# Row scatters from SBUF in place of lists in DRAM, and scores in three fp32r passes

## The reference, cut to what matters

```python
# attention, 16 heads of 16 features; kernel of 1 + s/4 + (s/4)^2/2, s = q.k
qf, kf = taylor_exp(q), taylor_exp(k)
A = jnp.tril(jnp.einsum('bhnd,bhmd->bhnm', qf, kf))
y = jnp.einsum('bhnm,bhme->bhne', A, v)
z = 1.0 / (jnp.einsum('bhld,bhld->bhl', qf, jnp.cumsum(kf, axis=2)) + EPS)
attn = (y * z[..., None]) @ Wo.T             # heads put side by side
# experts: 8, two for each token
top_w, top_i = jax.lax.top_k(xn @ Wg, 2)     # softmax over the two
y_e = (jax.nn.silu(xn @ W1[e]) * (xn @ W2[e])) @ W3[e]
moe = sum of the two chosen y_e, each times its weight
```

## Time and profile before

| | |
|---|---|
| median of 3 runs | 752.8 us (752.7 to 753.59) |
| profiled execution: time, span | 748.22 us, 746.5 us |
| PE busy, clock granted on average | 670.4 us (90%), 0.967 |
| DVE, ACT, POOL busy | 378.3, 318.9, 337.9 us |
| DMA moved | 46.77 MB, 63 GB/s |
| attention (to 389.8 us) and experts | 389.8 and 356.7 us |

### The profile page before, as it was taken

One profiled execution on the slowest core, in us unless ns is written; L12 is line 12 of the kernel. 1 busy time (PEld: TensorE's weight loads), 2 busy tenths in 40 slices (PEclk: granted clock), 3 DMA queues, 4 the chain that ended last, 5 costly groups with the idle time before them and its releaser, 6 DMA issues.

```text
span 746.5 us, 15613 instructions
## 1 busy us (share of the span) xinstructions
PE 670.4 (90%) x5315; PEld 502.1 (67%) x5315; DVE 378.3 (51%) x919; ACT 318.9 (43%) x468; POOL 337.9 (45%) x356
## 2 busy tenths in 40 slices
PE   3679999999998999887569999999999999999993
PEld 2435565656565655544258888888888888888882
DVE  4645656575756654354348744444444444444441
ACT  3355756566665656364237422333322333222330
POOL 1153544545352625243305655555545555545542
PEclk9899999999999999999679999999999999999997
DMA  6106053543516050003851233333333333333331
GB/s 211 37 1 86 17 32 97 40 104 38 107 31 84 16 43 16 15 2 42 252 225 29 52 59 58 58 59 58 58 54 55 51 59 59 58 54 55 58 52 21
DMA packets 37240, 46.77 MB, mean 63 GB/s; under 512 B 9520, under 2 KB 31424, under 8 KB 37168
## 3 DMA queue, kind: packets, MB, share of 16 engines
q1 hardware_dynamic: 21024, 25.71, 17.6%
q0 software_dynamic: 15712, 19.01, 15.8%
q10 hardware_dynamic: 432, 1.06, 0.4%
HBM read 27.50 MB, written 18.26 MB: 61 GB/s over the span
## 4 chain that ended last, share of the span: by engine, by line
PE 74%; DVE 12%; DMA 5%; issue 3%; another core or an unknown queue 2%; ACT 1%; POOL 1%; SPq 0%; DVEq 0%; POOLq 0%; ACTq 0%
PE banks L1007 26%; PE banks L1028 13%; PE banks L872 8%; PE banks L909 6%; PE banks L890 6%; PE banks L1016 4%; PE banks L953 3%; PE banks L918 3%; PE banks L938 2%; DMA lists_scr<-ids,slots 2%; DMA out<-yo,glist 2%; PE banks L996 2%; DVE yw L634 1%; DVE st L577 1%
## 5 line engine op out<-in xcount | busy, mean ns | idle before, releaser
L371 POOL TENSOR_SCALAR_AFFINE_SELECT T<-T 128x512 f32<-128x512 f32 x128 | 79.5, 637 | 173.3 <-ACT T L458 60.6
L411 POOL DMA_INDIRECT out<-yo,glist x71 | 114.1, 1607 | 81.0 <-DMA out<-yo,glist 39.0
L540 ACT ACTIVATE sTh<-banks 128x512 fp32r<-128x512 f32 x71 | 42.5, 598 | 193.6 <-PE banks L1016 193.6
L1007 PE MATMUL banks<-w12h,xgh 128*128 x284 | 118.7, 418 | 4.5 <-DVE xgl L821 4.5
L400 POOL DMA_INDIRECT xg<-xn_scr,glist x71 | 69.7, 981 | 106.7 <-DVE yo L833 94.8
L872 PE MATMUL banks<-Qs,Ks 32*128 32x512 f32 (+3 forms) x1024 | 100.5, 475 | 16.9 <-ACT T L463 8.3
L1007 PE MATMUL banks<-w12l,xgh 128*128 x284 | 112.4, 396 | 0.0
L1007 PE MATMUL banks<-w12h,xgl 128*128 x284 | 112.3, 396 | 0.0
L826 DVE TENSOR_TENSOR sTl<-banks,sTh 128x512 fp32r<-128x512 f32 x71 | 49.0, 691 | 116.7 <-ACT sTh L540 116.7
L450 ACT ACTIVATE T<-banks 128x1024 f32<-128x1024 f32 x64 | 62.0, 1021 | 53.1 <-PE banks L872 49.0
L872 PEld LDWEIGHTS banks<-Qs,Ks 32*128 32x128 f32 x1024 | 46.0, 187 | 51.6 <-issue 21.1
(11 more groups left out here) (157 smaller groups left out, 1133.4 us busy)
## 6 DMA issues: line engine op xcount, KB each, us to landing
w12r<-w SPq DMA_DIRECT2D x16, 512.0 KB, 8.2
xn_scr<-xb SPq DMA_DIRECT2D x8, 512.0 KB, 9.3
out<-xa SPq DMA_DIRECT2D x16, 256.0 KB
w3r<-w SPq DMA_DIRECT2D x8, 512.0 KB, 7.0
xa<-x SPq DMA_DIRECT2D x7, 512.0 KB, 4.4
xg<-xn_scr,glist POOLq DMA_INDIRECT x71, 2.8
out<-yo,glist POOLq DMA_INDIRECT x71, 3.8
lists_scr<-ids,slots POOLq DMA_INDIRECT x64
```

The source lines that it names most:

```text
L371: e.affine_select(out=v, in_=v, pattern=[[0, 4], [1, P]], compare_op=ALU.is_ge, fill=-1.0, base=0, channel_multiplier=-1).then_inc(s["g_mk ...
L411: e.indirect_dma_start(out, bass.IndirectOffsetOnAxis(glist[:, t:t + 1].bitcast(U32), 0), yo[:, t % 2, :], None, compute_op=ALU.add).then_ ...
L1007: i = e.matmul(banks[:, 2 * (t % 2) + m, :], a[:, k, :], w[:, bass.ds(expert[t] * 4 + (2 * k + m), 1), :], start=(k == 0 and n == 0), stop ...
```

## The change

**No lists in DRAM.** A row of xn, its eight gate weights and its token number now stand side by side in SBUF (`xb`, 272 words). POOL's `send` scatters each row to `xs_scr` by batch, expert and rank, twice, one indirect DMA for 128 rows, eight a batch; they stand singly between masks (`sends_after`). The stores of xn, the table, the wait on its entries and the read of the lists are gone. DVE works out which row of `xs_scr` each tile's row is (`tile_starts`, `tile_gaps`, `tile_rows`, `all_rows`, in the steps of batch 7). The scatter of results uses the row's own token number, copied with the weights (`xw`). Gates are worked out batch by batch.

**Scores.** q and k are kept as high and low parts, ACT making the high, DVE the low ones, and each group of columns takes three fp32r passes, in the same four row groups. Part 1 is 384 columns, part 2 twice 256 (where 128 would do for one).

**Beside it**: slots and DVE's work in them are arranged anew; buffers are laid out so that 8 weight units can come by batch 3 and the others one by one; the first loads are spread over two queues; the square root is a power on POOL; 36 transposes of the identity run on PE ahead of its first work; output projections of batch 7 stand between the first expert's products.

The diff, cut to its core:

```diff
+W12_WITH = {(1, 1): 0, (1, 2): 1, (2, 1): 2, (2, 2): 3, (3, 1): 4, (3, 2): 5, (4, 1): 6, (4, 2): 7, (7, 0): 8}
+def slot_b(n):
+    b, qd = divmod(n, 4)
+    if qd == 0:
+        steps = [("T", b, 0), ("c", b, 2)]
+    elif b == LAST:
+        steps = [("o", b - 1, qd - 1)] if qd < 3 else []
+    elif qd == 1:
+        steps = [("x", b + 1, 0), ("x", b + 1, 1)]
+    else:
+        steps = [("c", b + 1, 3 - qd)]
+    return steps + ([("t", (n - 1) // 4, (n - 1) % 4)] if n else [])
+def slot_c(n):
+    b, qd = divmod(n, 4)
+    if qd == 0:
+        return [("c", b, 3)] + ([("y", b - 1, 1)] if b else []) + [("r", b, 0)]
+    if b == LAST:
+        return [("y", b, 0), ("G", 0, 0)] if qd == 3 else []
+    steps = [("o", b - 1, qd // 2)] if b and qd != 2 else []
+    if qd == 3:
+        return steps + [("y", b, 0), ("C", b + 1, 0)]
+    return steps + [("v", b + 1, 2 * qd - 2), ("v", b + 1, 2 * qd - 1)]
...
+            def send(b, i0, i1):
+                if i0 == 0:
+                    number(b)
+                e.wait_ge(s["v_xn"], 4 * b + 4)
+                e.wait_ge(s["v_slots"], b + 1)
+                e.wait_ge(s["v_cw"], b + 1)
...
+                    e.indirect_dma_start(xs_d, bass.IndirectOffsetOnAxis(slots[:, k, 4 * b + blk:4 * b + blk + 1].bitcast(U32), 0),
+                                         xb[b % 2][:, blk, :], None).then_inc(s[f"d_xs{b % 2}"], 16)
...
-                    e.wait_ge(s["v_row"], 1)
-                    e.wait_ge(s["d_sl"], 16 * 2 * NB)
-                    e.indirect_dma_start(lists[:], None, table_rows,
-                                         bass.IndirectOffsetOnAxis(row[:, 0:1].bitcast(U32), 0)).then_inc(s["d_li"], 16)
...
+                    e.activation(Qh[k // 2][:], bank("c", b, k), ACT.Copy).then_inc(s["a_qh"], 1)
...
+                        e.activation(Kh[:, k // 2, h, :], bank("c", b, k), ACT.Copy, scale=km[:, h:h + 1]).then_inc(s["a_kh"], 1)
...
-                        i = e.tensor_scalar(Ks[:, k // 2, h, :], bank("c", b, k), km[:, h:h + 1], None, ALU.mult)
+                        i = e.scalar_tensor_tensor(Kl[k // 2][:, h, :], bank("c", b, k), km[:, h:h + 1],
+                                                   Kh[:, k // 2, h, :].bitcast(F32), ALU.mult, ALU.subtract)
...
-                jobs = (((0, 0, 512, 0),), ((1, 0, 384, 128), (3, 384, 128, 384)), ((2, 0, 256, 256),))[part]
-                        i = e.matmul(banks[:, r, c0:c0 + w], Ks[rr, g, h, jm * P:(jm + 1) * P], Qs[rr, g, q0:q0 + w],
-                                     start=True, stop=True)
+                jobs = (((0, 0, 512),), ((1, 0, 384),), ((3, 0, 256), (2, 256, 256)))[part]
+                for j, (jm, c0, w) in enumerate(jobs):
+                    for p, (k, q) in enumerate(((Kh[:, g, h], Qh[g]), (Kh[:, g, h], Ql[g]), (Kl[g][:, h], Qh[g]))):
+                        for r in range(4):
+                            i = e.matmul(banks[:, r, c0:c0 + w], k[rr, jm * P:(jm + 1) * P], q[rr, 512 - w:512],
+                                         start=(p == 0), stop=(p == 2))
...
+            for _ in range(WARM):
+                e.transpose(banks[:, 0, 0:P], ident[:], ident[:])
...
+            transpose_g(0)
+            step("y", LAST, 1)
+            expert_of(0)
+            up(0, 0)
+            step("o", LAST, 0)
+            up(0, 1)
+            step("o", LAST, 1)
+            transpose_g(1)
```

More of the change, by code:

```diff
@@ new lines, in build, with w3_hi @@
+        cmp = rq.take("cmp", 72 * 7, F32, (72, 7))
+        part = rq.take("part", P)
+        tf = rq.take("tf", 72)
+        cum = rq.take("cum", 72, F32, (NE + 1, NE))
+        gap = rq.take("gap", 64, F32, (NBATCH, NE))
+        cb = rq.take("cb", NE)
+        off = rq.take("off", NE)
+        sel = rq.take("sel", 64, F32, (NBATCH, NE))
+        cumt = rq.take("cumt", NE)
+        gapt = rq.take("gapt", NE)
+        rown = rq.take("rown", P)
+        lists = rq.take("lists", P)
+        def w3_hi(n, e):
+            return Region(A0 + 1024 * n, A0 + 1024 * e)
@@ new lines, in after_b, with after_c @@
+            def after_b(n):
+                b, qd = divmod(n, 4)
+                if n == NQ - 3:
+                    tiles()
+                elif n == NQ - 2:
+                    tile_rows(0)
+                elif qd == 1:
+                    gates(b)
+                if qd == 2 and (b, qd) in W12_LOW_WITH:
+                    w12_low(W12_LOW_WITH[b, qd])
+            def after_c(n):
+                b, qd = divmod(n, 4)
+                if n == 0:
+                    w_low(3, Wol, wo_r, Woh)
+                elif qd == 1 and b < NBATCH - 2:
+                    sums(b + 2)
+                elif qd == 2 and b < LAST:
+                    top(b + 1, 0)
+                    if b < NBATCH - 2:
+                        rsqrt(b + 2)
+                elif qd == 3 and b < LAST:
+                    both(b + 1)
+                elif qd == 0 and 0 < b < LAST:
+                    norm_x(b + 1)
+                elif n == NQ - 4:
+                    place_rows(LAST)
+                elif n == NQ - 3:
+                    tile_starts()
+                elif n == NQ - 2:
+                    tile_rows(1)
+                elif n == NQ - 1:
+                    experts()
+                if qd == 3 and (b, qd) in W12_LOW_WITH:
+                    w12_low(W12_LOW_WITH[b, qd])
```

768 lines of the change are left out of this document (393 added, 375 removed).

## The result

The changed kernel takes **706.85 us** (median of four runs, 703.08 to 707.29), the kernel before 752.75 in the same rounds (746.19 to 753.59): a ratio of 0.940, with a 95% interval of 0.934 to 0.946. Its profiled execution took 707.29 us with a span of 705.6. The forecast was 708 with a span of 701.5.

The account below looks back on a forecast made before the run. PE was taken to bound batches and experts, waits for list entries the passage between. Stage terms summed to 694.4 us, plus 7.1 for half the unexplained stalls: span 701.5, with 1.7 and 4.6 on top 708 us; range 692 to 730.

Parts of the forecast that it names:

- Rival (c): End of attention: a scatter among weight loads lands late, first gather 10 us later, 718 us in all; chance 0.08.
- The two stretches: Step 31 to the last product with v, forecast 7.1 us; from there to expert tile 1, 17.9 us.
- The stalls: Three unexplained idle times in or beside score steps, together 14.3 us; the forecast kept half, 7.1 us.
- Batches 1 to 6: Six attention batches, four steps each: 38.2 us a batch by the sum, 229 us together instead of 245.8.
- The score term: Scores of each of 32 steps: three fp32r passes take 2.6 us instead of 2.80, 6 us less in all.
- DVE loses four of these copies and gets six subtractions of 512 columns, about +1.5 us: DVE in a batch: masked k copies go, low-part subtractions come; with gates and offsets 30 of 38 us busy.
- step 1: Second step of a batch: 9.2 us of PE work plus some 1.6 us waiting for norm_x, 10.8 us.
- step 2: Third step of a batch: one projection c, transposes and two v, 8.2 + 0.3 us.
- Rival (a): Batches: DVE or ACT becomes the bound, 40.6 us a batch instead of 38.2, +16, 724 us; chance 0.12.
- Rival (f): Unexplained stalls don't shrink or come more often with three times the matmuls: +7 to +15, 715 to 723; chance 0.07.
- The start: Up to the first scores: x over two queues, fewer low parts first, k before q; 15.5 us instead of 20.86.
- Batch 0, steps 28 to 30, the experts: First batch 40.2 us instead of 49.7, steps 28 to 30 26 instead of 30.7, experts 358.7 instead of 356.7.

Follow-up runs that it names:

- the wait: The changed kernel with one wait added: POOL waits for all row scatters to have landed ahead of the last two masks; 707.56 us.
- the 4 byte entries: The changed kernel with each of the 64 row scatters followed by a scatter of 128 entries of 4 bytes to a DRAM tensor of its own; 724.31 us.

## Why the prediction was right, and where not

**The end: mechanism right, sizes near.** The wait for entries and the read back went, the first gather's wait took their place and cost 2.2 us of POOL and 2.6 of PE where the earlier trace rows had 14.95 + 6.09. Rival (c) falls: the rows landed 5.5 us after the last issue, among weight loads. The two stretches are 1.7 us each over the forecast. In the first, DVE's ninth W12 low part (1.6 us) and tile arithmetic stand ahead of copy_yw(30), and PE waits 2.0 us for yw; with that wait at 0.7 or none the stretch is 8.1 us in both cases, so 0.7 of the 1.7 goes with this wait (both of those runs have fp32 scores), and the chain of scores and squares is 1.0 longer than I had it. The same code took 9.5 us for this stretch in its second trace, so these tenths are not firm. In the second the gather came within half a microsecond of its place (334.8 us; 326.64 + 3.2 + 4.5 by the forecast), and tile 0 with the output projections took 11.4 us at a granted clock of 0.83, where I had 10.2.

**The stalls: wrong step, and the total right by luck.** I kept half of 14.3 us because I had no cause, and wrote that the forecast would be wrong if they came more than twice or not at all. They came not at all. The cause was in plain view as something else: the 64 scatters of 4 byte entries that the change removes. I priced those at 1.04 us of POOL each and a wait at the end; 4 byte against 512 byte entries shows 29.5 us for them in the kernel before without lists, 24.3 of it in batches 1 to 6, and taking them out gives 12.3 there. A figure that should have made me ask is the landing of SP's row store, 9.3 us for 512 KB on the profile's page, where x loads of the same size landed in 4.4; without entries, or with 512 byte ones, it lands in 3.0 or 3.1.

**Batches 1 to 6: 5.1 us too low.** The score term was right (2.54 against 2.6). The term that failed is "DVE loses four of these copies and gets six subtractions of 512 columns, about +1.5 us", hidden in 8 us of slack. Its busy time was right (28 us; I said 30), its effect was not: 7.3 us over the six batches, from two waits behind it, although DVE was busy for only 28 of 38.9 us. I had step 1 at 10.8 (measured 11.07) and step 2 at 8.5 (9.30), and step 2 is where Kl holds the bank. That the passes alone would not pay in full shows too: 3.5 us of the 6.2 that 0.26 us a step makes. Of the 11.7 us that these batches gained, the passes and the low parts together gave less than nothing (-3.8); the run without list entries gains 12.3 there alone.

**Rival (a)** has its mechanism in part (dependent chains on DVE, strictly in order) at a third of its price: PE's waits for DVE are 1.3 us a batch, where its own mark was over 4. **Rival (f)** falls with the stalls.

**The start: 1.5 us too low.** The projection waited for wqk, which landed 7.8 us after its issue behind x; behind the projection PE waited 2.0 us more for DVE's low part of q, the same low parts as in the batches. Both the landing and the clock change from run to run. In five profiled executions of this start code wqk landed after 6.1 to 7.8 us, and first scores came between 15.4 and 18.0. In two of the five (the wait, and the 4 byte entries) the projection ran partly at 1.2 GHz. With 512 byte entries it started at 10.18 us and was done by 13.3; with 4 byte ones it started at 11.54, was still at work from 13 to 15 us, and the granted clock was 0.50 (windows view, 512 first):

```profile
13.00:15.00 2.00, 0.34 (x2) 0.00 (x0) 1.69 (x3) 1.40 (x3) 0.00 (x0) 1.00 0.00 1
```

```profile
13.00:15.00 2.00, 2.00 (x6) 1.52 (x6) 0.30 (x1) 0.75 (x2) 0.00 (x0) 0.50 0.07 24
```

The pitch of the projection's matmuls is 0.23 us at 2.4 GHz in the one and 0.43 at 1.2 in the other. First scores came at 15.4 and 17.6: of these 2.2 us, 1.4 are the later start of the projection, and the clock has at most the other 0.8. Ahead of the projection PE had run the transposes of the identity and of x, to 9.7 us, and then waited 0.44 us in the one and 1.87 in the other. In the trace of the changed kernel it waited 2.19 us there and kept 2.4 GHz, so this wait alone does not tell which it will be. In the kernel before the pitch was 0.43 us until 18.1 us, as at 1.2 GHz and as the forecast took it, though the windows view gives a granted clock of 1.00 there; that trace has no record of the clock before 18.2 us.

**Batch 0, steps 28 to 30, the experts** came within 0.7 us. The terms inside them were not tested one by one. The power on POOL took 1.05 us, about in the middle of the bounds of 0.2 and 2 and not at the low end that I took.

## What to carry to other kernels

A stall without a cause, in a kernel with many small writes to DRAM, is to be tested and not halved: put larger entries in their place and look at the landing times of the other queue. Before a matmul is split into parts, ask what the parts cost on the engine that makes them, in its order and not in its busy time: here three fp32r passes with the low parts lose to plain fp32 by 1%. A wait that moves costs nothing if what stands behind it waits for the same event, as the wait ahead of the last masks showed. Time the kernel before again beside every run: its median moved from 749 to 766 us between sessions, more than most effects here.

## What I had not expected of the hardware

- 8192 writes of 4 bytes in place of as many of 512 bytes cost 29.5 us of 730, in the kernel before without lists, and stretched 55 of 11400 packets of another queue, with a median of 0.05 us, to between 3 and 6.1 us. The Trainium skill (DMA: Bandwidth & Descriptors, section Why small descriptors are slow (HBM only)) gives a fixed overhead for each packet. By that a small entry costs about what it costs itself; here it is the others that pay, and in the changed kernel nobody did (724.31 us with 4 bytes, 722.38 with 512).
- fp32 score groups of 32 rows fit four passes for three in fp32r, and yet the step is only 2.80 against 2.54 us. Some 0.2 us at each part's start and end are the same in both, and the fp32 groups have 1280 columns where the fp32r ones have 1408.
- First scores of the same start code differ by up to 2.6 us between five profiled executions: the landing of wqk differs by 1.7 us, and two had PE at 1.2 GHz in the first projection.
